# A decoder's layer norms outside the attention stream: the reciprocal root as a power on GpSimd instead of a square root on ScalarE and a reciprocal on VectorE

## What is computed

```python
def _layernorm(x, axis=-1, eps=1e-05):
    m = jnp.mean(x, axis=axis, keepdims=True)
    v = jnp.var(x, axis=axis, keepdims=True)
    return (x - m) / jnp.sqrt(v + eps)

x = _layernorm(x + _L0_attn_ref(x, ...))       # banded attention, then its own norm with gamma, beta, then a GELU FFN
x = _layernorm(x + _L0_xattn_ref(x, ctx, ...)) # causal cross attention
x = _layernorm(x + _L0_ffn_ref(x, ...))        # 8 LoRA experts on one FFN, top 2
x = _layernorm(x + _L1_attn_ref(x, ...))       # full attention
x = _layernorm(x + _L1_xattn_ref(ctx, ctx, x, mask, ...))
x = _layernorm(x + _L1_ffn_ref(x, ...))        # 8 experts, top 2
```

## Time and profile before

| | |
|---|---|
| median of 3 runs | 3046.66 us (3045.34 to 3050.92) |
| the profiled execution, its own time | 3047.43 us |
| its span in the trace | 3045.7 us |
| TensorE busy | 2741.8 us, 90% of the span |
| VectorE busy | 2004.5 us, 66% |
| ScalarE busy | 1614.2 us, 53% |
| GpSimd busy | 302.6 us, 10% |
| granted TensorE clock, mean of the span | 0.948 of full speed |

### The profile page before, as it was taken

How to read it: one execution, slowest core, us unless ns; L and a number is a source line. 1 busy time by engine, 2 the same in 40 slices (tenths; PEclk the granted TensorE clock), 3 DMA queues, 4 the chain that set the end, 5 groups by cost and what they waited for, 6 DMA issues and landing times. The chain is left out here.

```text
span 3045.7 us, 85811 instructions
## 1 busy us (share of the span) xinstructions
PE 2741.8 (90%) x35674; PEld 1361.9 (45%) x35675; DVE 2004.5 (66%) x4025; ACT 1614.2 (53%) x3062; POOL 302.6 (10%) x446
## 2 busy tenths in 40 slices
PE   6798978999988988999999999999999998289992
PEld 3575643444545553233333333333343433057672
DVE  4443148888844236889899998999999994222224
ACT  2224223666663222477777777877777778023331
POOL 2117011000110002111000000000000000300004
PEclk9898988999998999799999999999999999699996
DMA  5523032011010004221221221111111110710103
GB/s 160 130 45 110 1 98 82 16 27 40 3 38 13 0 1 136 82 67 39 64 53 29 64 54 38 47 46 57 46 46 46 46 46 2 283 36 31 34 31 91
DMA packets 115181, 173.65 MB, mean 57 GB/s; under 512 B 20139, under 2 KB 90684, under 8 KB 114452
## 3 DMA queue, kind: packets, MB, share of 16 engines
q1 hardware_dynamic: 109012, 160.12, 18.3%
q0 software_dynamic: 5824, 8.49, 0.9%
HBM read 127.63 MB, written 40.51 MB: 55 GB/s over the span
## 5 line engine op out<-in xcount | busy, mean ns | idle before, releaser
L1402 DVE TENSOR_REDUCE d_part_max<-d_ps_m 128x1 f32<-128x512 f32 (+1 forms) x1964 | 1107.6, 622 | 61.1 <-PE d_ps_m L1389 40.3
L1720 ACT ACTIVATE d_prob<-d_ps_s 128x512 f32<-128x512 f32 x1856 | 958.7, 604 | 229.9 <-PE d_ps_s L1579 228.1
L1389 PE MATMUL d_ps_m<-k_st,q_st 97*32 97x512 bf16 (+1 forms) x5296 | 465.9, 356 | 0.4 <-DVE d_part_max L1402 0.4
L1579 PE MATMUL d_ps_s<-q_st,k_st 98*32 98x512 bf16 x5104 | 442.7, 382 | 13.0 <-ACT d_prob L1720 10.7
L784 DVE TENSOR_REDUCE x_part_max<-x_att_ps_m 128x1 f32<-128x512 f32 (+2 forms) x578 | 305.4, 581 | 45.4 <-PE x_att_ps_m L760 19.7
L1025 ACT ACTIVATE x_att_prob<-x_att_ps_s 128x1024 f32<-128x1024 f32 (+3 forms) x296 | 258.2, 921 | 129.9 <-PE x_att_ps_s L906 77.7
L1595 PE MATMUL d_ps_o<-d_prob,a_values 128*32 128x512 f32 x2048 | 264.1, 591 | 0.0
L1579 PEld LDWEIGHTS d_ps_s<-q_st,k_st 98*32 98x32 bf16 x5104 | 136.5, 96 | 265.3 <-ACT d_prob L1720 165.6
L1389 PE MATMUL d_ps_m<-q_st 97*32 97x512 bf16 (+1 forms) x2560 | 225.2, 357 | 0.0
L1389 PEld LDWEIGHTS d_ps_m<-k_st,q_st 97*32 97x32 bf16 x5296 | 140.8, 96 | 173.9 <-issue 70.3
L1595 PE MATMUL d_ps_o<-d_prob,x_values 128*32 128x512 f32 x1664 | 214.7, 592 | 0.2 <-ACT d_prob L1720 0.2
(11 more groups left out here) (337 smaller groups left out, 3304.4 us busy)
## 6 DMA issues: line engine op xcount, KB each, us to landing
k_st<-parts_k SPq DMA_DIRECT2D x90, 256.0 KB, 5.3
k_st<-parts_k SPq DMA_DIRECT2D x90, 208.0 KB, 4.6
l_w<-in_l_w SPq DMA_DIRECT2D x16, 1024.0 KB, 14.5
q_st<-parts_q SPq DMA_DIRECT2D x48, 256.0 KB, 4.6
q_st<-parts_q SPq DMA_DIRECT2D x192, 64.0 KB
q_st<-parts_k SPq DMA_DIRECT2D x30, 256.0 KB
q_st<-parts_k SPq DMA_DIRECT2D x30, 208.0 KB
parts_q<-a_proj_parts SPq DMA_DIRECT2D x16, 384.0 KB, 2.5
```

Source lines behind the costliest of these rows:

```text
L1389: mm = pe.matmul(bank[q:q + COLUMNS, 0:w], self.query(s, h, ROW_MASK + 1, a * P + q, COLUMNS), self.key(s, h, ROW_MASK + 1, k, w), start=T ...
L1402: dve.tensor_reduce(self.part[:, h * QT + a, i:i + 1], bank[:, 0:w], AX.X, ALU.max).then_inc(s_read, 1)
L1579: mm = pe.matmul(ps_s[n % len(ps_s)][k:k + COLUMNS, :], maxima.key(s, h, ROW_MAX + 1, kt * P + k, COLUMNS), maxima.query(s, h, ROW_MAX + 1 ...
L1720: act.activation(prob[:, p % 2, h, :], ps_s[n % len(ps_s)][:, :], ACT.Exp, scale=scale).then_inc(s_prob, 1)
```

## The change

The square root on ScalarE and the reciprocal on VectorE are replaced by two operations on GpSimd: an add of epsilon (still counted on `s_std`) and a power with the exponent -0.5 from a constant of four columns (counted on `s_inv`, for which `scale` waits). The calls of `root` move from ScalarE's lists to GpSimd's. `eps` is still filled, and no longer read.

```diff
     c["eps"] = sb("eps", [P, 1], F32)
+    c["power"] = sb("power", [P, 4], F32)
...
             fill(c["eps"][:, :], EPS)
+            fill(c["power"][:, :], -0.5)
...
-    def root(self, act, quad):
+    def root(self, pool, quad):
         q = slice(quad * 4, quad * 4 + 4)
-        act.wait_ge(self.s_mv, 4 * (quad + 1))
-        act.activation(self.std[:, q], self.mean_var[:, q, 1], ACT.Sqrt,
-                       bias=self.cst["eps"][:, 0:1]).then_inc(self.s_std, 1)
+        pool.wait_ge(self.s_mv, 4 * (quad + 1))
+        pool.tensor_scalar(self.std[:, q], self.mean_var[:, q, 1], EPS, None, ALU.add).then_inc(self.s_std, 1)
+        pool.wait_ge(self.s_std, quad + 1)
+        pool.tensor_tensor(self.inv[:, q], self.std[:, q], self.cst["power"][:, :], ALU.pow).then_inc(self.s_inv, 1)
 
     def scale(self, dve, quad):
-        q = slice(quad * 4, quad * 4 + 4)
-        dve.wait_ge(self.s_std, quad + 1)
-        dve.reciprocal(self.inv[:, q], self.std[:, q]).then_inc(self.s_inv, 1)
         dve.wait_ge(self.s_inv, quad + 1)
...
@@ close_attention, GpSimd @@
-            if gain is not None:
-                for t in range(NT):
-                    norm.apply_gain(pool, t)
+            norm.root(pool, 0)
+            for quad in range(NT // 4):
+                if quad + 1 < NT // 4:
+                    norm.root(pool, quad + 1)
+                if gain is not None:
+                    for t in range(4 * quad, 4 * quad + 4):
+                        norm.apply_gain(pool, t)
...
@@ close_attention, ScalarE @@
-                if t % 4 == 1 and t > 4:
-                    norm.root(act, t // 4 - 1)
                 if t >= LAG:
                     norm.copy_out(act, t - LAG)
-            norm.root(act, NT // 4 - 1)
...
@@ gelu_ffn, GpSimd @@
+            for quad in range(NT // 4):
+                norm.root(pool, quad)
...
@@ gelu_ffn, ScalarE @@
-                if c >= 2:
-                    norm.root(act, c - 2)
             for c in range(NQ):
-                if c >= NQ - 2:
-                    norm.root(act, c)
...
@@ lora_ffn, ScalarE @@
-                if c >= 2 and f == 1:
-                    norm.root(act, c - 2)
...
             for c in (NQ - 2, NQ - 1):
-                norm.root(act, c)
...
@@ lora_ffn, GpSimd @@
+        @block.gpsimd
+        def _(pool):
+            for quad in range(NT // 4):
+                norm.root(pool, quad)
...
@@ expert_ffn, ScalarE @@
-            for quad in range(NT // 4):
-                norm.root(act, quad)
...
@@ expert_ffn, GpSimd, in the loop of gathers over t @@
+                if t % 4 == 3 and t > 4:
+                    norm.root(pool, t // 4 - 1)
+            norm.root(pool, NT // 4 - 1)
```

## The result

With the change the kernel takes **3053.91 us** in the median of 13 runs (3049.51 to 3061.22); 13 runs of the kernel before, beside them, gave 3046.66 us. The ratio is **1.0024, 95% interval 1.0015 to 1.0032**: about 7 us slower, where 3057.2 was forecast. A second set of 12 runs gave 3053.65 us and 1.0023 (1.0013 to 1.0032).

What follows compares the result with a forecast made beforehand. TensorE's expert products, with GpSimd's gathers and their landing, were taken to end the kernel, GpSimd's order of work counting there. Terms +5.0 - 3.0 + 2.2 - 1.3 + 1.4 - 0.2 + 6.4 = +10.5 us gave 3057.2 us, range 3051.0 to 3066.0.

Steps and rivals of the forecast that it cites:

- Price of a root: All norms: an unhidden root costs 0.9 us more (1.47 against 0.58 us); a hidden one saves VectorE 0.18 us.
- First closing: End of first attention: four roots join GpSimd's queue of bias adds and gains, which ends the stage; +5.0 us.
- GELU stage: TensorE-bound stage: table load, square root and reciprocals go, last root is ready earlier; -3.0 us.
- Second closing: End of second attention: root 0 late behind bias adds, last root unhidden, some given back; +2.2 us.
- Routing: Way to the routing's end: the exponential's table load goes; -1.3 us.
- LoRA stage: Two unhidden roots with TensorE waiting, 0.9 us each, less 0.4 us for a table load; +1.4 us.
- Start of the stream: Ahead of the first exponentials: a 1.28 us table load goes, partly hidden beside TensorE; -0.2 us.
- Tail: Expert stage: roots queue among and behind GpSimd's 32 gathers, the last root unhidden; +6.4 us.
- only shift: Long attention stages between the norms: hold none of these roots, so they move in time without changing length.
- GpSimd and VectorE shut each other out: Rival: exclusion, or powers costing more among gathers, puts terms at upper ends; +14 to +19, some 3063 us; chance 0.18.
- each removed load gives back twice its length: Rival, ScalarE's table loads on the path: another 3.2 us back, +7.3, some 3054 us; chance 0.06.
- The not-slower rival: All nine of ScalarE's removed loads were on the path; +2.2, some 3048.9 us; chance 0.04.

Runs made afterwards that it cites:

- closes_old: Changed kernel with the roots of both closings back on ScalarE: 3056.42 us, ratio 1.0028; run once more (closes_old_again): 3053.22 us, ratio 1.0021.
- best_filled: best with four memsets that do nothing for the result on VectorE at the start of the GELU stage: 3036.93 us, ratio 0.9969.
- best: Kernel before, with GpSimd powers only for all GELU-stage and the first two LoRA-stage roots, and an early exponential in the routing: 3042.55 us, ratio 0.9986.
- more_powers: Changed kernel plus unused powers on GpSimd: three behind each GELU-stage root, one behind each expert-stage root; one execution of 3059.48 us.

## Why the prediction was right

The side was right, and 3053.9 lies in the range of 3051.0 to 3066.0, 3.3 us under the forecast. By its own steps, with the means of the table:

- **Price of a root**: 0.9 us for an unhidden one. Held to the hundredth: TensorE's two waits in the LoRA stage went from 4.03 and 2.71 us to 4.92 and 3.61.
- **First closing +5.0**: +5.8. GpSimd paces it and its own queue is what grew, as said; the idle ahead of root 1 was 3.51 us. The gains ended at 289.0, 3 us beyond the forecast place, 2 us of it because the stage began later.
- **GELU stage -3.0**: -2.7.
- **Second closing +2.2**: +2.2.
- **Routing -1.3**: -1.4. **LoRA stage +1.4: +0.4.** The term was right by itself: where the routing's load still stands ahead of the stage, it takes 183.4 us with square roots (4 profiles) and 185.0 with powers (both of `closes_old`), +1.6. Where that load is gone too, it takes 183.3 (6 profiles), and this 1.7 us is what the sum had left out. TensorE stands idle for 1.9 us ahead of the stage, not 3.3, and its granted clock in the first 8 us is 0.80 to 0.82, not 0.66 to 0.73 (rows below).
- **Start of the stream -0.2**: can't be told; the stream's length varies by 4 us between profiles (1349.0 to 1353.1).
- **Tail +6.4**: +6.0, with its marks: three breaks (two among the gathers, the third behind them), waits of about 3 us, 54.7 us from the first gather where "some 56" was said.

The windows are the first 8 us of the LoRA stage in the kernel before (load on the routing's path, square roots), in `closes_old_again` (load, powers) and in the changed kernel (no load, powers); the granted clock is the last number but two:

```profile
956.10:964.10 8.00, 8.00 (x13) 3.46 (x14) 0.62 (x3) 0.69 (x1) 0.00 (x0) 0.66 0.38 115
957.00:965.00 8.00, 8.00 (x13) 3.47 (x14) 0.62 (x3) 0.69 (x1) 0.00 (x0) 0.68 0.44 116
960.30:968.30 8.00, 7.98 (x15) 3.61 (x16) 0.63 (x3) 0.77 (x2) 0.00 (x0) 0.80 0.41 115
```

The shorter wait doesn't ensure the higher clock: of the eight profiles with 1.9 us, seven have 0.80 or more, but best_filled has 0.61, and its LoRA stage took 182.8 us where that of best took 181.3.

These terms sum to +10.3 us, the start of the stream left out (10.7 forecast without it), and +7.3 was measured. **The step that failed is the one by which the stages between the norms "only shift", and a stage's gain ends at its barrier.** They don't only shift: the projection behind the GELU stage gained 2.4 us by TensorE's clock, the head of the LoRA stage 1.7 us by the same (within the terms above), the second attention lost 2.5 us by VectorE's idle time, and the projection behind the LoRA stage is 1.2 us shorter. There the granted clock of the first 10 us is 0.78 to 0.80 at powers and 0.69 to 0.71 at square roots, but best, with 0.86 and 111.2 us, doesn't fit, so that its cause stays open. Together the three untouched stages give -1.1 us, which leaves 1.9 us that no term holds; the stream alone varies by 4 us between profiles. That the total came within 3.3 us of the forecast is in part luck: these errors cancelled.

Of the rivals, the one in which GpSimd and VectorE shut each other out had the right observation (3.22 us against 1.81 us) and the wrong culprit: 128x256 operations of GpSimd double the scalings' time, 128x4 powers don't touch it (1.35 and 1.38 us with powers beside them). The rival in which each removed load gives back twice its length named +7.3, some 3054 us, which is the measured number, and for another reason: where a load lay on the path, the routing gained 1.4 us for 1.28, with nothing beside the load on ScalarE; the further 1.7 us came one stage later, by TensorE's clock. The not-slower rival fell with the result.

## What to carry to other kernels

Moving a small operation to the least busy engine costs what that engine's queue is worth at that place: ask in each stage who releases the barrier, and leave the operation off that engine there, however idle it is on average. Where the receiving engine has nothing to do, the move is good even for a slower instruction, and a table load is as well moved into a wait as removed. And before believing a few microseconds in a kernel of this length, look for instructions whose idle time ends by nothing ("issue"), above all where an engine's loop jumps back, and at the clock over the next border: both are moved by edits that have nothing to do with them.

## What was not expected of the hardware

- **An engine's loop can stall at its jump back, by how many instructions stand ahead of it.** VectorE's list in the second attention is a loop over the head groups (`dve.Fori` in `attend`), and the idle times begin where it jumps back. In the ten profiles with 501 or 505 instructions ahead, the first instruction of the loop comes 2.9 to 3.1 us after the branch; in the four with 509 it comes 0.35 us after it. Each idle time holds one packet of the instruction queue q14, which starts 0.2 to 0.7 us into it; in the profiles with 509 that queue moves nothing between 182 and 267 us from the attention's start. The rows below are of best: the loop's branch, the first instruction of its two rounds (first and last start), and windows over the two idle times, in which the packets start at 698.5 and 701.2:

```profile
L1093 DVEq COMPARE_BRANCH  x2: 59/61/63, 697.5 to 804.0; - x2
L1093 DVEq FUSED_REGOPS  x2: 70/70/70, 595.4 to 700.4; - x2
...
698.10:700.50 2.40, 1.79 (x32) 0.76 (x24) 0.03 (x2) 0.42 (x1) 0.49 (x2) 1.00 0.01 3
700.80:703.00 2.20, 0.35 (x8) 0.12 (x8) 0.00 (x1) 1.71 (x3) 0.23 (x1) 0.82 0.52 135
```

  So VectorE waits for its own instructions. That they come late because the next group's stacks are loaded, as the last expectation had it, is refuted for the first idle time: in all ten profiles the instruction packet is the only one that starts in it (DMA 0.01 busy above), and the transfers of the stacks begin only later. The Trainium skill's page Runtime: NRT & Kernel Launch, section "Instruction fetch mechanics", says that an engine refills its instruction memory in blocks of 16 KiB, 256 instructions, that the cost of a border is mostly hidden, and that a taken branch to a target outside the two blocks held has to wait for a fetch. The trace agrees with the last: these idle times stand behind a taken branch. That four or eight instructions fewer push the loop's start over the border of a block is an inference, and so is why four cost more than eight: in best VectorE ran one instruction (0.29 us) between the two idle times. Where the borders lie isn't shown, and the packets of q14 are of 8 KB here.
- **Such a stall costs more than its length**, since TensorE waits behind VectorE (0.95 and 2.55 us in best) and its clock falls: with the two idle times of 4.6 us together, the attention of best is 5.2 us longer than the mean of those with 509. The windows of best show the clock, 0.87 and then 0.50:

```profile
700.00:703.00 3.00, 0.35 (x8) 0.12 (x8) 0.29 (x2) 2.43 (x3) 1.01 (x2) 0.87 0.38 99
703.00:706.00 3.00, 2.26 (x36) 1.23 (x40) 2.91 (x5) 0.31 (x1) 0.00 (x0) 0.50 0.87 245
```

- **VectorE is slowed by some of GpSimd's instructions and not by others.** Four scalings of 128x256 take 1.35 us alone or beside powers of 128x4, and 2.71 us beside adds of 128x256, though a power (1.04 us) is longer than an add (0.72 us). That the size of what GpSimd moves makes the difference is an inference; a large power or a small add was not tried. The Trainium skill's page SBUF — State Buffer, section "SBUF: two separate sides", has GpSimd and VectorE hold the port pair that they share for an instruction's whole length. The trace agrees for the adds, and disagrees for the powers: three of them, back to back, held nothing up (the group at 410.60 in `more_powers`).
